# Butterfly weights: the four high stages as matrix products, in 72 pieces over the recurrence's steps

## The reference

```python
x = x + attn(_layernorm(x), ...)    # a linear recurrence over the first axis (4 steps), in 64-wide blocks
x = x + xattn(_layernorm(x), ctx, Wq, Wk, Wv, Wo)   # 16 heads over 77 context rows
x = x + ffn(_layernorm(x), ...)
...
def butterfly(y, weights, dim):      # dim = 2048, 11 stages
    for stage in range(weights.shape[0]):
        s = 2 ** stage
        nb = dim // (2 * s)
        yr = y.reshape(*lead, nb, 2, s)
        a, b = yr[..., 0, :], yr[..., 1, :]
        w = weights[stage].reshape(nb, s, 2, 2)
        na = w[..., 0, 0] * a + w[..., 0, 1] * b
        nb2 = w[..., 1, 0] * a + w[..., 1, 1] * b
        y = jnp.stack([na, nb2], axis=-2).reshape(*lead, dim)
    return y
h = x @ W_exp + b_exp                # 512 -> 2048
h = gelu(butterfly(h, up_weights) + up_bias)
y = butterfly(h, down_weights) @ W_con + b_con + down_bias
```

## Time and profile before

| | us |
|---|---|
| median of three runs | 2365.08 (2363.87 to 2365.98) |
| the profiled execution | 2366.6 |
| its span, first to last instruction | 2364.8 |

### The profile page before, as it was taken

One profiled execution on the slowest core, in us unless ns is written; L12 is line 12 of the kernel. 1 busy time (PEld: TensorE's weight loads), 2 busy tenths in 40 slices (PEclk: granted clock), 3 DMA queues, 4 the chain that ended last, 5 costly groups with the idle time before them and its releaser, 6 DMA issues.

```text
span 2364.8 us, 42243 instructions
## 1 busy us (share of the span) xinstructions
PE 2226.1 (94%) x15752; PEld 1943.3 (82%) x15752; DVE 1769.8 (75%) x2969; ACT 1293.1 (55%) x2832; POOL 557.2 (24%) x619
## 2 busy tenths in 40 slices
PE   8877789999999999969999999999999999999998
PEld 4777668778777877748998998988989989989898
DVE  5999668878878887755875867857858758678567
ACT  2998556666667666543644635535536446355343
POOL 3788222222222322200030030020210300300203
PEclk9888879999999999989999999999999999999999
DMA  8555702332332232256568677676685686776765
GB/s 329 192 178 189 263 2 77 116 124 77 108 116 94 85 119 90 95 182 219 172 219 267 199 218 227 208 262 179 212 263 177 214 266 200 223 221 210 225 188 177
DMA packets 190883, 424.47 MB, mean 179 GB/s; under 512 B 27342, under 2 KB 64718, under 8 KB 190286
## 3 DMA queue, kind: packets, MB, share of 16 engines
q1 hardware_dynamic: 190696, 421.94, 55.1%
HBM read 331.29 MB, written 90.60 MB: 178 GB/s over the span
## 4 chain that ended last, share of the span: by engine, by line
PE 65%; DVE 16%; ACT 11%; issue 4%; DMA 3%; POOL 1%; SPq 0%; DVEq 0%; ACTq 0%; POOLq 0%
PE ps L416 52%; PE ps L1805 5%; ACT es L982 5%; PE ps L1773 2%; DVE gl L1178 2%; DVE G L1530 2%; DVE st L1149 2%; DVE ptl L1178 1%; DVE wc_s L1178 1%; PE ps L1784 1%; DMA xa<-in_x 1%; DVE rsum L1401 1%; ACT wc_h L939 1%; DVE rmax L1390 1%; ACT pth L957 1%
## 5 line engine op out<-in xcount | busy, mean ns | idle before, releaser
L416 PE MATMUL ps<-ring,gh 128*128 128x256 f32 x3584 | 654.4, 285 | 12.6 <-DVE gl L1178 12.5
L416 PEld LDWEIGHTS ps<-ring,gh 128*128 128x128 f32 x3584 | 558.0, 192 | 16.9 <-DVE gl L1178 15.7
L416 PE MATMUL ps<-xth,ring 128*128 128x512 f32 x1792 | 554.6, 390 | 4.2 <-ACT U L1066 4.2
L416 PE MATMUL ps<-ring,gl 128*128 128x256 f32 x1792 | 506.8, 283 | 0.0
L416 PEld LDWEIGHTS ps<-xth,ring 128*128 128x128 f32 x1792 | 337.4, 188 | 74.7 <-issue 4.6
L1054 ACT ACTIVATE gh<-G 128x512 fp32r<-128x512 f32 x384 | 237.2, 629 | 212.4 <-PE ps L416 212.1
L416 PE MATMUL ps<-xtl,ring 128*128 128x512 f32 x896 | 349.5, 390 | 0.0
L416 PEld LDWEIGHTS ps<-ring,gl 128*128 128x128 f32 x1792 | 343.4, 192 | 0.0
L1178 DVE TENSOR_TENSOR gl<-G,gh 128x512 fp32r<-128x512 f32 x384 | 278.8, 739 | 57.2 <-ACT gh L1054 55.6
L759 POOL TENSOR_TENSOR es<-es,rinv 128x308 f32<-128x308 f32 x256 | 180.2, 735 | 456.5 <-DVE rinv L1405 456.5
L1470 DVE TENSOR_TENSOR U<-ps,U 128x512 f32<-128x512 f32 (+1 forms) x168 | 137.3, 817 | 169.5 <-PE ps L416 166.9
(11 more groups left out here) (212 smaller groups left out, 4646.0 us busy)
## 6 DMA issues: line engine op xcount, KB each, us to landing
ring<-wup_scratch SPq DMA_DIRECT2D x224, 512.0 KB, 3.8
ring<-wdn_scratch SPq DMA_DIRECT2D x224, 512.0 KB, 3.6
X<-x_scratch SPq DMA_DIRECT2D x32, 1024.0 KB, 8.5
xa<-in_x SPq DMA_DIRECT2D x16, 1024.0 KB, 5.5
x_scratch<-xa SPq DMA_DIRECT2D x16, 1024.0 KB, 4.3
x<-x_scratch SPq DMA_DIRECT2D x16, 1024.0 KB, 5.6
x_scratch<-x SPq DMA_DIRECT2D x16, 1024.0 KB, 4.3
out_x<-X SPq DMA_DIRECT2D x16, 1024.0 KB, 6.3
```

What stands on the lines that cost most here:

```text
L416: mm = pe.matmul(bank, a, b, start=first and i == 0, stop=last and i == n - 1, skip_group_check=go_on)
```

## The change

The high butterfly stages become matrix products as well. For that a second grouping of the 2048 rows is used: rows p*16 + j with p = 0 to 127 for a fixed j, where the four high stages act inside the group. Their combined weights are a 128x128 matrix for each j (`mq`). VectorE (up) and GpSimd (down) build them by choosing and multiplying weights that are loaded repeated over the partitions (`pick_up`, `join_up`, `pick_down`, `join_down`, `high_matrix`). Between the low and the high stages the rows are regrouped through DRAM.

The work is cut into 72 pieces, which TensorE, ScalarE and SyncE run between the four parts of each step: 16 low up (LU), 4 low bias (BL), 16 high up with the transpose in the product (UH), 16 high down (DH), 4 high bias (BH), 16 low down (DL). Each piece is one PSUM bank, copied by ScalarE to one of eight stages and stored by SyncE. After piece 15 SyncE loads `xg` (4 MB) and `yg` (4 MB), after piece 51 `yd` (4 MB), and small bias loads after 23 and 59. The elementwise butterfly, the low up products in the setup and the folding stretch are gone. `xa` holds five groups, with one semaphore for each; the recurrence's products use two PSUM banks; group g+4 is loaded in step g. Two of the first four queries run in step 15. The values are projected in three row tiles (128, 128 and 52 rows).

```diff
+        LU, BL, UH, DH, BH, DL = 0, MC, MC + 4, 2 * MC + 4, 3 * MC + 4, 3 * MC + 8
+        PIECES = 4 * MC + 8
+        PER_GROUP = [6, 6, 4, 4, 4, 4, 4, 4, 4, 4, 4, 4, 4, 5, 5, 6]
+        xslot = lambda g: (g + 3) % XS
...
 @@ SyncE, setup
+            sp.dma_start(ident[:, :], ident_in).then_inc(ident_loaded, 16)
             sp.dma_start(cT[:, :, :], ctxT).then_inc(kctx_loaded, 16)
             sp.dma_start(wk[:, :, :], rows(wkT)).then_inc(kctx_loaded, 16)
             sp.dma_start(wv[:, :, :], rows(wvT)).then_inc(wv_loaded, 16)
+            by_row = lambda w: w.rearrange("q s k e -> q (s k e)").unsqueeze(0).broadcast_to([MC, P, HIS * (MC // 2) * 4])
+            sp.dma_start(hw_up[:, :, :, :, :, :], by_row(hi_up)).then_inc(hw_loaded[0], 16)
             sp.dma_start(wgu[:, :], lo_up).then_inc(lo_loaded[0], 16)
+            load_x(0)
+            sp.dma_start(wgd[:, :], lo_dn).then_inc(lo_loaded[1], 16)
+            load_x(1)
             for q in range(4):
+                sp.dma_start(xu[:, 4 * q:4 * q + 4, :], wexp_v[:, 4 * q:4 * q + 4, :]).then_inc(xu_loaded[q], 16)
             sp.dma_start(be[:, :], bexp).then_inc(bias_loaded, 16)
+            sp.dma_start(ubg[:, :], upbias.rearrange("(l j) c -> c l j", j=MC), allow_slow_non_contiguous=True).then_inc(bias_loaded, 16)
             sp.wait_ge(kv_lo, KC)
             sp.dma_start(kt_d[0], raw(kth[:, :, :])).then_inc(kt_stored, 16)
             sp.dma_start(kt_d[1], raw(ktl[:, :, :])).then_inc(kt_stored, 16)
+            load_x(2)
...
             sp.wait_ge(kt_stored, 32)
+            load_x(3)
+            load_x(4)
+            sp.dma_start(hw_dn[:, :, :, :, :, :], by_row(hi_dn)).then_inc(hw_loaded[1], 16)
+            sp.wait_ge(v_stored, 64)
...
 @@ SyncE, steps
+            def regrouped(n):
+                if n == BL - 1:
+                    staged(BL)
+                    by_group = wl_d.rearrange("(p j) n -> p j n", j=MC)
+                    for q in range(4):
+                        sp.dma_start(xg[:, 4 * q:4 * q + 4, :], by_group[:, 4 * q:4 * q + 4, :]).then_inc(xg_loaded[q], 16)
+                    sp.dma_start(yg[:, :, :], wcon.rearrange("(p j) n -> p j n", j=MC)).then_inc(yg_loaded, 16)
...
+            for g in range(NG):
+                for c in range(KC):
+                    for n in pieces_at(g, c):
+                        piece_out(n)
+                        regrouped(n)
+                    if c == 1:
+                        if g:
+                            stored(sp, x1_stored, g - 1)
+                        if g and g + 4 < NG:
+                            load_x(g + 4)
...
+                sp.wait_ge(x1_ready, KC * g + KC)
+                sp.dma_start(x1_st[g], xa[:, xslot(g), :, :]).then_inc(x1_stored, 16)
...
 @@ ScalarE
+            def piece_back(n):
+                act.wait_ge(piece_pe, n + 1)
+                bank = ps[:, 6 + n % 2, :]
+                after(act, stage_out[n % STAGES], 16 * (n // STAGES))
+                rows = 1 if BL <= n < UH or BH <= n < DL else P
+                ins = A(stage[n % STAGES][0:rows, :], bank[0:rows], ACT.Copy)
+                ins.then_inc(piece_act, 1)
...
+            for g in range(NG):
+                for c in range(KC):
+                    for d in {0: (0, 1), 1: (2, 3)}.get(c, ()):
+                        if g + 1 < NG:
+                            hi1_piece(g + 1, d)
+                    if c > 1 and g + 2 < NG:
+                        apply1(g + 2, range(2 * c - 4, 2 * c - 2))
...
+                    for n in pieces_at(g, c):
+                        piece_back(n)
...
 @@ VectorE
+            def pick(out, first, second, b):
+                picks(V.tensor_scalar(out, first, bits[:, b, 0:1], None, ALU.mult))
+                return V.scalar_tensor_tensor(out, second, bits[:, b, 1:2], out, ALU.mult, ALU.add)
...
+            bit_masks()
             for f in range(KC):
+                pick_up(f)
                 dve.wait_ge(kv_hi, f + 1)
                 sub(ktl[:, f, :], ps[:, 4 + f, 0:NB * L], kth[:, f, :]).then_inc(kv_lo, 1)
...
+                if g + 2 < NG:
+                    stats1(g + 2, [lows[0], lows[1], None, None])
+                    lows = lows[2:]
...
+                for c in range(KC):
+                    n = KC * g + c
+                    dve.wait_ge(s5_done, n + 1)
...
+                    V.tensor_tensor(xs, xs, ps[:, 4 + n % 2, :].rearrange("p (b t n) -> p b t n", b=2, t=T), ALU.add).then_inc(x1_ready, 1)
+                    if c == 0:
+                        for low in lows:
+                            low()
...
 @@ TensorE
+                if n < BL:
...
+                    mm = pe.matmul(bank, tup[:, c * P:(c + 1) * P], xu[:, c, :], start=True, stop=True)
...
+                elif n < DH:
...
+                    for i in range(KC):
+                        cols = slice(i * P, (i + 1) * P)
+                        mm = pe.matmul(bank[:, cols], xg[:, j, cols], mq[0][:, j, :], start=True, stop=True)
...
+            pe.wait_ge(ident_loaded, 16)
+            pe.wait_ge(r_lo, NB)
+            t1(0)
+            pe.wait_ge(kv_lo, KC + VT)
+            for g in range(NG):
+                if g + 1 < NG:
+                    t1(g + 1)
...
+                for c in range(KC):
+                    for n in pieces_at(g, c):
+                        piece(n)
+                    out1(g, c)
+                    if g == NG - 1 and c > 1:
...
+                        query(ps[:, c - 2, :], c - 2).then_inc(pre_pe, 1)
```

More of the change, by code:

```diff
@@ new lines, in decoder_layer @@
+    stage = [nc.alloc_sbuf_tensor_at(f"stage{i}", [P, D], F32, offset=at) for i, at in enumerate(stage_at)]
+    paths = [r1.put(n, [P, MC, MC], F32) for n in ("path_up", "path_dn")]
+    be = r1.put("be", [P, MC], F32)
+    ubs = r1.put("ubs", [P, MC], F32)
+    bg = r1.put("bg", [P, MC], F32)
+    ubg = r1.put("ubg", [P, MC], F32)
+    bits = r1.put("bits", [P, HIS, 2], F32)
+    same = r1.put("same", [P, LG], F32)
+    sel, tree = [], []
+    for m, n in enumerate(("up", "dn")):
+        sel.append([r1.put(f"sel_{n}{b}", [P, MC, 1 << (b if m == 0 else HIS - 1 - b), 2], F32) for b in range(HIS)])
+        tree.append([r1.put(f"tree_{n}{i}", [P, MC, 4 << i], F32) for i in range(2)])
@@ L161, in decoder_layer @@
+    rest = [hw_up] + [nc.alloc_sbuf_tensor_at(f"rest{i}", [P, MC, HIS, MC // 4 >> i, 2, 2], F32, offset=half_at(i % 2, 0))
+                      for i in range(HIS - 1)]
+    rt = Region(half_at(1, 1))
     sm = rt.put("sm", [HS, 32], F32)
@@ L571, in load_wc @@
             def load_wc(n):
[L572 to L573 removed]
+                for i, out in enumerate(stage_out):
+                    sp.wait_ge(out, stage_turns(PIECES, i))
                 after(sp, wc_stored, 32 * n)
@@ L667, in _, with low_paths @@
             link = Link(pool, lo_step)
-            def paths(w, up, loaded, ready):
+            def low_paths(w, up, loaded, ready, stages=range(1, LOS)):
                 pool.wait_ge(loaded, 16)
-                for s in range(1, LOS):
+                for s in stages:
                     n = 2 ** s
@@ new lines, in _, with pick @@
+            picks = Link(pool, pool_sel)
+            def pick(out, first, second, b, shape):
+                mask = [bits[:, b, v:v + 1].unsqueeze(2) for v in range(2)]
+                if len(shape) == 4:
+                    mask = [m.unsqueeze(3) for m in mask]
+                nc.gpsimd.tensor_tensor(out, first, mask[0].broadcast_to(shape), ALU.mult)
+                picks(nc.gpsimd.tensor_tensor(second, second, mask[1].broadcast_to(shape), ALU.mult))
+                picks(nc.gpsimd.tensor_tensor(out, out, second, ALU.add))
@@ new lines, in join_down @@
+            def join_down():
+                n, first = 2, sel[1][HIS - 1][:, :, 0, :]
+                for s, out in zip(range(HIS - 2, -1, -1), (tree[1][0][:, :, :], tree[1][1][:, :, :], paths[1][:, :, :])):
+                    new = out.rearrange("p j (h i) -> p j h i", i=2)
+                    old = first.unsqueeze(3).broadcast_to([P, MC, n, 2])
+                    ins = nc.gpsimd.tensor_tensor(new, old, sel[1][s][:, :, :, :], ALU.mult)
+                    if s:
+                        picks(ins)
+                    first, n = out, 2 * n
+                pool.wait_ge(path_ready, 1)
+                ins.then_inc(path_ready, 1)
@@ new lines, in join_up @@
+            def join_up():
+                n, first = 2, sel[0][0][:, :, 0, :]
+                for s, out in enumerate((tree[0][0][:, :, :], tree[0][1][:, :, :], paths[0][:, :, :])):
+                    new = out.rearrange("p j (o l) -> p j o l", o=2)
+                    old = first.unsqueeze(2).broadcast_to([P, MC, 2, n])
+                    ins = V.tensor_tensor(new, old, sel[0][s + 1][:, :, :, :].rearrange("p j l o -> p j o l"), ALU.mult)
+                    if 2 * n < MC:
+                        picks(ins)
+                    first, n = out, 2 * n
+                ins.then_inc(path_ready, 1)
@@ L1733, in turn3 @@
```

(4 more changed lines are left out.)

650 lines of the change are left out of this document (286 added, 364 removed).

## The result

The changed kernel takes 2391.1 us in the median of four runs (2389.4 to 2392.5), the kernel before 2364.5 beside it (2363.7 to 2366.0): a ratio of 1.0106, with a 95% interval of 1.0093 to 1.0118. It is 26.7 us slower. The ratios and intervals here are those of the record; they can differ by up to 0.12% from the quotient of the two medians (1.0113 here). 2350 was forecast, the range ended at 2367. The profiled span went from 2364.8 to 2390.8 us.

The account below looks back on a forecast made before the run. VectorE was taken to set the 11.5 us step, TensorE after the change. First scores: 94.5 + 158 + 11 + 3 = 266.5, 15 us before 281.35, giving 2350 us in the median; range 2333 to 2367.

Parts of the forecast that it names:

- the first cut: Busy times by stage before the change: only the time of the first score product, 281.35 us, would move.
- rival B: TensorE's clock in the steps stays at a mean of 0.87, costing 27 us more: 2376 us; chance 0.13.
- where the queue stalls: Step 5: group 7's load stands in SyncE's queue behind 8.4 MB of xg and yg and x1's store.
- the load of group 2: Setup and step 0: lands at 58 us (54 to 72), harmless below 61, worth 9 us at 72.
- aside on its bias load: Group 2's wait in the setup: at some 10.5 ns a packet the bias load takes 1.3 us instead of 4.
- Attention and feed-forward unchanged, 2083: Behind the first scores: code that the diff leaves alone keeps its 2083 us.
- the list of what would be wrong: Signs against the forecast: pieces over 1.15, clock below 0.92, hole missing or repeated, attention and feed-forward changing their 2083 us.
- Step 0 ends at 71.4: Setup and step 0: with 8 us for VectorE's choice of up weights, step 0 ends at 71.4 us.
- x7 at +32, hole 11: Step 5: group 7's load lands 32 us after the third step's end, costing 11 us with half clock.
- Step 14: 3: Step 14: x1's first reload is late behind 4 MB of yd, costing 3 us (0 to 8).
- Queries 11.1; the last split 1.4: End of the recurrence: queries take 11.1 us and the last split 1.4 before the first scores.

Follow-up runs that it names:

- v_pitch: The changed kernel with the rows of the value scratch 640 elements apart instead of 512; 2375.9 us (ratio 1.0044).
- before_v_rows: The kernel before with only the change's DRAM layout of the value scratch (308 contiguous rows, batch after batch); 2380.1 us (ratio 1.0055).
- gpsimd_later: The changed kernel with GpSimd's products of the up paths behind the first rstd instead of ahead of it; 2386.1 us (ratio 1.0083).
- after_again: The changed kernel once more, unaltered, beside three others on one chip; 2392.6 us (ratio 1.0115).
- yg_early: The changed kernel with the 4 MB of yg loaded in four quarters as its buffer comes free, in steps 0 to 2; 2389.1 us (ratio 1.0106).
- no_up_loads: The changed kernel without the loads of xg and yg (8.4 MB), the high pieces reading xu instead; 2370.1 us (2364 to 2378).
- trips_spaced: The changed kernel with value scratch rows 640 apart, GpSimd's rsqrt early, xg, yg and yd in quarters and pieces respread over the steps; 2364.7 us (ratio 0.9995).
- all_moves: The changed kernel with scratch rows 640 apart, earlier rsqrts, the tail moved, reload ahead of stores, and xg, yg, yd loads rescheduled; 2365.0 us (ratio 0.9999).

## Why the prediction was wrong

Right were: the first cut, with VectorE's 11.5 us step before; TensorE as the bound after, with pieces of 0.86 to 0.97 us against 0.86 and 1.0, and steps of 10.7 to 10.8 (11.7 for the two with the bias pieces, 11.2 forecast); the granted clock of 1.00 in them, against rival B; where the queue stalls, and how long x1's store takes there; the load of group 2, which held nothing up. (It landed at 53.2, ahead of the 54 to 72. The aside on its bias load is wrong: 1.3 us divides the 10.5 ns a packet of the Trainium skill, DMA: Bandwidth & Descriptors, by 16 engines, but the page has it from 64 packets in 0.67 us on all of them; 2,048 packets would be an estimated 21 us by it. The load landed 10.2 us after its issue and 0.4 behind the load ahead of it, which bears out neither.) The direction was wrong, and five assumptions of the sum made it so.

- **"Attention and feed-forward unchanged, 2083."** 2096.8, and 13 to 15 of the 26.7 us. I compared the code behind the first scores and not the layout of the buffer that it reads: the change to the values' projection, priced at one row tile saved, rewrote `v_d`. v_pitch and before_v_rows show it from both sides. No rival held it either; only the list of what would be wrong named it.
- **"Step 0 ends at 71.4."** 80.4. The choice of weights was priced at 8 us by VectorE's own durations; GpSimd ran beside it on the same buffers' side, and the last key split came at 35.1 instead of 22.3. gpsimd_later gave back 7.5 us at that split, 6.3 at the end of step 0 and, over the whole, about 5. The other 2.7 are by the chain the wait for `hw_up`, 13.7 us from issue to landing; no run moved it.
- **"x7 at +32, hole 11."** +37.8 us from the step's end, because SyncE waited 3.8 us for piece stores and not 1, and took another 2.5 to issue the five big loads ahead of x1's store; the store itself and the load took 25.65 and 5.8 against 25.5 and 5.5. VectorE waited 15.3 us, and step 5 took 27.3 instead of 10.8, so the term is 16.5. The mechanism was right, the size 5.5 short.
- **"Step 14: 3."** Steps 13 and 14 took 15.9 and 23.9 us, where 11.5 each and the 3 were forecast: 13.7 more. VectorE waited 10.3 us in step 14 for x1, and TensorE 2.5 for the first quarter of `yd` in step 13, with a half clock behind each wait. I counted on the step's own slack and two products for a chain of two stores and one reload behind 4 MB. (The trace of after_again has 11.6 and 26.2: the split between the two steps isn't fixed.)
- **"Queries 11.1; the last split 1.4."** Two of the four queries fell into step 15, so 5.6 + 1.4 = 7 were left behind its last sum. It was 9.9: the statistics of the second x1 group (2.5), their rstd (1.0) and the copy (2.9) stand ahead of the last query split. Moved, they cost as much behind.

Together 9.0 + 5.5 + 13.7 + 2.9 = 31.1 before the first scores, and the other steps came 3.6 short of the forecast, 2.8 of it in step 15: 266.5 became 294.0.

The prediction priced each transfer by itself at 390 GB/s, and the steps' own traffic at nothing. That traffic was 182 GB/s and went to 294 to 319 with the piece stores (3.1 MB in 10.7 us). It did not make the hole of step 5 longer, for x1's store took what was forecast; the time from issue to landing of the ordinary stores of x1 before the attention rose from a median of 4.3 us to 8.3, and SyncE waits for each. The stall forecast was a matter of order, and of one place. The runs say that no order tried hides the 8.4 MB of `xg` and `yg`, and the traces say that most of what is left of their cost comes from SyncE falling behind, in steps where TensorE itself is not held up by it until `yd` is due. For `yd` neither is tested.

Not settled: why yg_early's median lies 4 us above its own profiled execution, and why no_up_loads varies over 14 us. trips_spaced and all_moves equal the kernel before; no version that computes the reference was faster.

## What to carry to other kernels

Work moved from a busy engine to an idle one takes its intermediate results along: add up the bytes for each step, old and new, before any single transfer is priced, and follow the engine that issues them: what it waits for, and whether it is still ahead of the step that it serves. A DMA share near 1 in a step whose bound engine is busy throughout costs nothing by itself; the same step without the transfer tells. When a buffer's layout changes, every reader of it is part of the change, in whatever stage. And a wait read from a trace is worth at most the distance to the next one: here single moves against waits of 10 to 15 us gave 0 to 8, and only a run without the transfers told what they cost.

## What the runs showed of the hardware

- The same small load costs SyncE 0.80 us to issue with a row step of 512 floats and 0.40 with 640 or 2048, where each row is cut into four parts 128 floats apart.
- A VectorE operation over 32 elements took 4.54 us beside a GpSimd product over up to 2048 elements, and 0.25 without it.
- A store of a megabyte that took a median of 4.3 us in the steps of the kernel before (DMA share 0.51) took 8 to 10 in the steps of all_moves, at a DMA share of 0.84 to 0.96; TensorE was busy in all of those steps.
- With and without the transfers of `xg` and `yg`, at DMA shares of 0.96 and 0.89 or of 1.02 and 0.80, the same steps took the same time.
